# A transformer layer on one core: the first pass over the scores on 64 rows, two heads side by side in the row halves of TensorE

## The chip, the cores and the metric

The kernel runs on one core of a Trainium2 chip. The metric is the time of one execution on the device in microseconds, the median of several runs.

## The reference

One layer with a LayerNorm ahead of each half: `x = x + attention(LN(x))`, then `x = x + ffn(LN(x))`, with x of 2 x 2048 x 256 in float32. Attention has 16 heads of 16 dimensions, is causal, and q and k go through a rotary embedding:

```python
q = split_heads(x @ Wq.T + bq)          # k and v likewise
q, k = (rope(q), rope(k))
att = jnp.einsum('bhqd,bhkd->bhqk', q, k) / 4.0
att = jax.nn.softmax(jnp.where(mask, att, -jnp.inf), axis=-1)
y = jnp.einsum('bhqk,bhkd->bhqd', att, v)
```

The feed-forward part (256 to 704 to 256) rounds the input and the weights of each product to a block-wise FP4 grid: `fp4_linear(silu(fp4_linear(x, w_gate)) * fp4_linear(x, w_up), w_down)`.

## The kernel before, in words

**Tiling.** 4096 tokens are 32 tiles of 128 and 8 chunks of 512 (four a sequence). A unit `u` is a chunk of queries and a group of four heads: 8 x 4 = 32 units, in the order of chunks. A step is a unit and one tile of 128 keys, 320 in all. Everything is float32 but the score products. For these, q and k are each split into three bf16 parts (high, middle, low), and six products of parts stand below each other in the contraction: `Q_TERMS` and `K_TERMS` name them, 6 x 16 = 96 rows (`TERM_ROWS`), and 3 more rows (`ROWS` = 99) subtract the row's maximum, also in three parts, against three rows of ones.

**First pass (L766).** For each piece (unit, query tile, up to 512 keys; one head, or several where few keys are left) TensorE multiplies the 96 rows into one bank of PSUM, and on the diagonal adds the mask with an identity matmul (L770). VectorE reduces the bank to a maximum (L1096). When all pieces of a unit are done, VectorE splits the negated maxima in three (`place_maxima`, L1107 to L1122), TensorE turns them (L870), ScalarE copies them out (L1026), and SyncE places them with three DMAs in rows 96 to 98 of `q_mem` (L716).

**Second pass.** L784 computes the scores with keys on the partitions from all 99 rows, the maximum thus already subtracted; L787 adds the mask; ScalarE takes the exponential (L1037) into `prob`; and P·V (L805) multiplies by V, four heads side by side in four column quarters of the array (128 rows by 32 columns each), as float32 in two passes, so eight matmuls a step, all into bank 7 (`O_BANK`).

**The rest.** Projections (L817 with `WqkvT`), RoPE on GpSimd (L1362 to L1371) and in the first chunk on VectorE for every second tile, the splitting (`hi`, `mid`, `lo`), transposes of the parts (L863), their store to DRAM by SyncE (L687, one DMA of 768 KB for two tiles) and the deals, twelve DMAs a unit that bring each part into its rows of `q_mem` and `k_mem` (L698, L707). Feed-forward tiles (L812, L817, L906, L915) run between the attention of later chunks.

**What sets the order.** A planner (`Plan`) rehearses the whole program before it is built, with a duration for each step written in the code, and gives every step a number; each engine's program then emits its steps in that order (`in_time`). `Plan.through` also picks the bank for each use: of those free, the one that comes free first. `rehearse_maxima` keeps at most `S_IN_FLIGHT` = 4 pieces of the first pass between matmul and reduction, `rehearse_probabilities` at most three of the second. TensorE waits, in `take`, until the bank's last user has drained it. A first pass may run up to two units ahead of the second, since two sets of maxima exist.

## Time and profile before

| | before |
|---|---|
| median of 3 runs | 1479.56 us (1475.61 to 1482.19) |
| the profiled execution | 1482.4 us, of which the profile's span is 1480.6 |
| mean granted TensorE clock | 0.969 |
| TensorE matmul busy | 1364.8 us (92%), 8500 instructions |
| VectorE busy | 1111.1 us (75%), 2300 |
| ScalarE busy | 819.1 us (55%), 1724 |
| GpSimd busy | 496.4 us (34%), 552 |

Busy time is the time in which an instruction of the engine is under way. Matmuls are pipelined and their ends modelled, so what one matmul costs TensorE is read from the distance between starts. PE is TensorE, PEld its weight loads, DVE VectorE, ACT ScalarE, POOL GpSimd, SP SyncE. L766 is line 766 of the kernel.

### The profile page before, as it was taken

What the parts mean: (1) busy time and instruction counts of PE and PEld (TensorE: products, weight loads), DVE (VectorE), ACT (ScalarE), POOL (GpSimd) and SP (SyncE); (2) the same over time, 40 slices, a digit from 0 to 9 for tenths busy, and PEclk for the clock granted to TensorE, in tenths of its full rate; (3) what the DMA queues carried; (4) which work ended last, traced back from release to release, by engine and by line L of the source; (5) the groups of instructions that cost most, each with busy time, mean ns of one, the idle gap of its engine ahead of it and who ended that gap; (6) DMA issues with size and microseconds to landing.
All of it is one profiled execution on the core that took longest, in us unless ns stands there. A gap on an engine that the chain in (4) does not pass through costs nothing.

```text
span 1480.6 us, 23285 instructions
## 1 busy us (share of the span) xinstructions
PE 1364.8 (92%) x8500; PEld 675.7 (46%) x8500; DVE 1111.1 (75%) x2300; ACT 819.1 (55%) x1724; POOL 496.4 (34%) x552
## 2 busy tenths in 40 slices
PE   5669899899989999999989999999999999999986
PEld 2344344454444444444435545454345444444454
DVE  4688996889768797887527887878887987874373
ACT  1446466555556565655674555565665655667510
POOL 5743333424333451212212352542121122123345
PEclk9789999999999999999999999999999999999997
DMA  4323203111111101100011202120001000000000
GB/s 92 100 79 113 61 1 96 42 46 33 33 33 44 40 26 37 30 8 30 27 30 51 79 5 77 46 66 8 23 30 37 23 8 9 9 8 8 26 1 18
DMA packets 78457, 56.63 MB, mean 38 GB/s; under 512 B 12924, under 2 KB 78076, under 8 KB 78332
## 3 DMA queue, kind: packets, MB, share of 16 engines
q1 hardware_dynamic: 78344, 55.15, 12.8%
q8 instruction: 67, 1.10, 0.3%
q14 instruction: 46, 0.38, 0.1%
HBM read 37.95 MB, written 16.78 MB: 37 GB/s over the span
## 4 chain that ended last, share of the span: by engine, by line
PE 65%; DVE 21%; DMA 4%; issue 3%; ACT 3%; SPq 2%; POOL 2%; DVEq 0%; ACTq 0%; POOLq 0%
PE bank L817 15%; PE bank L805 14%; PE bank L784 12%; PE bank L766 11%; DVE piece_max L1096 10%; PE bank L915 5%; DMA a_mem<-in_L_attn_x 3%; ACT prob L1037 2%; PE bank L812 1%; PE bank L906 1%; PE bank L770 1%; PE bank L787 1%; DVE c_mem L1174 1%; PE bank L863 1%; DVE c_mem L1166 1%
## 5 line engine op out<-in xcount | busy, mean ns | idle before, releaser
L1037 ACT ACTIVATE prob<-bank 128x512 f32<-128x512 f32 (+3 forms) x1280 | 627.7, 537 | 411.4 <-PE bank L784 242.3
L1096 DVE TENSOR_REDUCE piece_max<-bank 128x1 f32<-128x512 f32 (+3 forms) x1120 | 703.9, 662 | 100.6 <-PE bank L766 56.6
L766 PE MATMUL bank<-k_mem,q_mem 96*128 96x512 bf16 (+3 forms) x1280 | 430.1, 352 | 18.6 <-DVE piece_max L1096 10.3
L784 PE MATMUL bank<-q_mem,k_mem 99*128 99x512 bf16 (+3 forms) x1280 | 434.9, 353 | 7.4 <-DVE piece_max L1096 5.7
L805 PE MATMUL bank<-prob,V 128*32 128x512 f32 (+3 forms) x2560 | 303.3, 546 | 2.4 <-ACT prob L1037 1.4
L784 PEld LDWEIGHTS bank<-q_mem,k_mem 99*128 99x128 bf16 x1280 | 123.8, 98 | 226.2 <-issue 140.9
L1324 POOL TENSOR_TENSOR c_mem<-c_mem 128x256 f32<-128x256 f32 (+2 forms) x72 | 82.4, 1145 | 407.9 <-DVE c_mem L1178 407.9
L766 PEld LDWEIGHTS bank<-k_mem,q_mem 96*128 96x128 bf16 x1280 | 125.8, 99 | 160.6 <-issue 71.1
L787 PE MATMUL bank<-mask_kq,ident_h 128*128 128x128 bf16 x512 | 110.7, 221 | 0.0
L770 PE MATMUL bank<-mask_qk,ident_h 128*128 128x128 bf16 x512 | 101.4, 224 | 0.0
L805 PEld LDWEIGHTS bank<-prob,V 128*32 128x32 f32 x2560 | 50.9, 109 | 97.1 <-issue 60.3
L1362 POOL TENSOR_TENSOR a_mem<-a_mem,sin_t 128x256 f32<-128x256 f32 x54 | 42.6, 810 | 138.6 <-DVE a_mem L1229 138.6
L817 PE MATMUL bank<-WqkvT,a_mem 128*128 128x512 f32 (+1 forms) x216 | 87.2, 528 | 0.8 <-ACT a_mem L998 0.6
L1327 POOL TENSOR_TENSOR c_mem<-c_mem 128x256 f32<-128x256 f32 (+2 forms) x72 | 82.7, 1148 | 3.6
L915 PE MATMUL bank<-WdT,c_mem 128*128 128x256 f32 x348 | 81.2, 383 | 1.2 <-ACT c_mem L1077 1.1
L817 PE MATMUL bank<-WgT,c_mem 128*128 128x352 f32 x232 | 81.3, 475 | 0.0
L817 PE MATMUL bank<-WuT,c_mem 128*128 128x352 f32 x232 | 79.0, 463 | 0.0
L1330 POOL TENSOR_TENSOR c_mem<-c_mem 128x256 f32<-128x256 f32 (+2 forms) x72 | 70.4, 978 | 3.9
L915 PEld LDWEIGHTS bank<-WdT,c_mem 128*128 128x128 f32 x348 | 64.7, 190 | 14.4 <-issue 4.7
L1382 POOL TENSOR_TENSOR c_mem<-c_mem,out_bias 128x256 f32<-128x256 f32 x29 | 21.0, 726 | 145.1 <-DMA c_mem<-in_L_attn_x 145.1
L1017 ACT ACTIVATE parts<-bank 128x1024 bf16<-128x1024 bf16 (+1 forms) x64 | 51.3, 812 | 25.9 <-PE bank L863 20.1
L787 PEld LDWEIGHTS bank<-mask_kq,ident_h 128*128 128x128 bf16 x512 | 50.6, 99 | 28.9 <-issue 5.6
(136 smaller groups left out, 1463.3 us busy)
## 6 DMA issues: line engine op xcount, KB each, us to landing
parts_dram<-parts SPq DMA_DIRECT2D x16, 768.0 KB, 4.3
q_mem<-parts_dram SPq DMA_DIRECT2D x192, 64.0 KB, 2.3
k_mem<-parts_dram SPq DMA_DIRECT2D x192, 64.0 KB, 2.3
c_mem<-in_L_attn_x SPq DMA_DIRECT2D x29, 128.0 KB, 2.1
out<-c_mem SPq DMA_DIRECT2D x29, 128.0 KB, 1.7
a_mem<-in_L_attn_x SPq DMA_DIRECT2D x27, 128.0 KB, 2.9
q_mem<-max_rows SPq DMA_DIRECT2D x96, 4.0 KB
k_mem<-in_L_attn_x SPq DMA_DIRECT2D x8, 128.0 KB, 2.9
```

The lines of the kernel that those rows point to most:

```text
L766: m = pe.matmul(o, q_rows(u)[0:TERM_ROWS, h, i * P:(i + 1) * P], k_rows(k0 // CHUNK, g)[0:TERM_ROWS, h, k0 % CHUNK:k0 % CHUNK + keys], sta ...
L770: m = pe.matmul(o[:, keys - P:keys], ident_h[:, :], mask_qk[:, :], start=False, stop=True)
L784: mm = pe.matmul(b[:, off:CHUNK], k_rows(j // TPC, g)[:, h, (j % TPC) * P:(j % TPC + 1) * P], q_rows(u)[:, h, off:CHUNK], start=True, stop ...
L787: mm = pe.matmul(b[:, off:off + P], ident_h[:, :], mask_kq[:, :], start=False, stop=True)
L805: mm = pe.matmul(O[32 * h:32 * h + 32, off:CHUNK], V[:, of % V_SLOTS, j % TPC, v0:v0 + 32], prob[:, (GROUP * m + h) % NP, off:CHUNK], star ...
L817: m = pe.matmul(b[:, 0:width], src[:, d * P:(d + 1) * P], w[:, d, lo:lo + width], start=(d == 0), stop=(d == DK - 1))
L915: m = pe.matmul(b[:, 0:D], hT[0:DOWN[j], j * P:(j + 1) * P], WdT[0:DOWN[j], j, :], start=(j == 0), stop=(j == len(DOWN) - 1))
L1037: act.activation(prob[:, n % NP, off:CHUNK], bank_of("st", n)[:, off:CHUNK], ACT.Exp, scale=SCALE).then_inc(drained("st", n)[0], 1)
L1096: dve.tensor_reduce(piece_max[:, u % 2, h0:h0 + len(heads), slot], src.rearrange("p (h k) -> p h k", k=keys), AX.X, ALU.max).then_inc(drai ...
L1324: pool.tensor_tensor(a, a, b, ALU.add).then_inc(done, 1)
L1327: pool.tensor_tensor(a, a, b, ALU.subtract).then_inc(done, 1)
L1330: pool.tensor_tensor(dst.rearrange("p (n f) -> p n f", f=FP4_BLOCK), a.rearrange("p (n f) -> p n f", f=FP4_BLOCK), v["scale"][0:rows, 0:nb ...
```

## The change

The first pass leaves two of the six products out (those with a low part), so it works on 64 rows: high x high, middle x middle, high x middle and middle x high. The second pass keeps all six. Since what the first pass finds is only subtracted inside the exponential and divides out again, the result stays what it was. Of the four heads of a group, heads 0 and 1 keep these 64 rows in partitions 0 to 63 and heads 2 and 3 in partitions 64 to 127; two matmuls, one in each half of the array's rows, go into two neighbouring banks, and one reduction takes both banks. A batch holds all four heads: two such pairs in a row, thus four banks, or one pair where two heads' keys fit in a bank. The masks of a batch follow after its matmuls.

Around that: the rows move (`BLOCK_AT`, `MAX_AT`); heads 2 and 3 have 29 rows of zeros in the second pass, which VectorE clears once; q, k, their weights and bias are laid out with the two heads of a pair innermost (`h=2`), so RoPE and the copies of weights go over other strides; the parts are stored by 14 DMAs of 64 KB for two tiles, and the deals take blocks of 32 rows by two heads; the maxima are placed with two DMAs. The planner knows pairs of banks (`pairs`, `take`), charges 70 ns for each change of the array's mode, counts 470 and 1800 ns instead of 550 and 1600 for a DMA's turn and landing, and prefers a batch by 1500 ns that can begin directly behind a P·V.

```diff
-S_IN_FLIGHT, ST_IN_FLIGHT = 4, 3
+S_IN_FLIGHT, ST_IN_FLIGHT = 2, 3
...
-HANDOVER_NS, DMA_TURN_NS, DMA_NS = 130, 550, 1600
+HANDOVER_NS, DMA_TURN_NS, DMA_NS, MODE_NS = 130, 470, 1800, 70
...
+BLOCK_AT = ((0, 32, 64), (64, 96, 0))
+MAX_AT = (96, 32)
+ROWS = (99, 128)
+ZEROS = (32, 64)
+PAIR_ROWS = ((0, 64), (64, 128))
...
+        if engine == "pe":
+            ns += MODE_NS * (mode != self.mode)
+            self.mode = mode
...
+    def pairs(self):
+
+        return [[b, b + 1] for b in self.bank_free if b % 2 == 0 and b in self.spare and b + 1 in self.spare]
...
-        for n, (u, i, heads, k0, keys, slot, masked) in enumerate(pieces):
-            yield [("deal k", u, 5)] + ([("place", u - 2, 2)] if u >= 2 else [])
-            if n >= S_IN_FLIGHT:
-                yield [("drain", "s1", n - S_IN_FLIGHT)]
...
+            for n in batch:
+                if n >= S_IN_FLIGHT:
+                    yield [("drain", "s1", n - S_IN_FLIGHT)]
+                yield plan.pairs
+                free.append(plan.take(("s1", n), min(plan.pairs(), key=lambda two: max(plan.bank_free[b] for b in two))))
+            yield free
+            for n in batch:
+                heads = pieces[n][2]
+                plan.do("pe", ("s1", n), 0.427 * len(heads) * keys + 10, *needs, *free, ("masks",), mode="rows")
...
+    plan.start(rehearse_maxima(), lambda begins: 1500 if plan.mode == "columns" and begins <= plan.engine_free["pe"] else SOONER_NS["s"])
...
+                for n, (o, part, d, row) in enumerate(stores):
...
+                    sp.dma_start(dst.rearrange("b r h t -> b (r h) t"),
+                                 parts[:, (part * 2 + o) * DK + d, :]).then_inc(parts_stored, 16)
...
-                        m = pe.matmul(o, q_rows(u)[0:TERM_ROWS, h, i * P:(i + 1) * P],
-                                      k_rows(k0 // CHUNK, g)[0:TERM_ROWS, h, k0 % CHUNK:k0 % CHUNK + keys],
-                                      start=True, stop=not masked)
...
+                    for n in batch:
+                        take("s1", n)
+                        b = plan.bank["s1", n]
+                        for j, h in enumerate(pieces[n][2]):
+                            for a in range(2):
+                                lo, hi = PAIR_ROWS[a]
+
+                                m = pe.matmul(bank[b + a][:, j * keys:(j + 1) * keys],
+                                              q_heads(u)[lo:hi, 2 * a + h, i * P:(i + 1) * P],
+                                              k_heads(k0 // CHUNK, g)[lo:hi, 2 * a + h, k0 % CHUNK:k0 % CHUNK + keys],
+                                              start=(j == 0), stop=not masked)
...
-                    dve.tensor_reduce(piece_max[:, u % 2, h0:h0 + len(heads), slot],
-                                      src.rearrange("p (h k) -> p h k", k=keys), AX.X,
...
+                    src = banks[:, b:b + 2, 0:some * keys].rearrange("p a (h k) -> p a h k", h=some)
+                    dve.tensor_reduce(of_tile[:, :, heads[0]:heads[0] + some], src, AX.X,
                                       ALU.max).then_inc(drained("s1", n)[0], 1)
...
+                dve.memset(q_mem[ZEROS[0]:ZEROS[1], :, 2:4, :], 0.0).then_inc(q_zeroed, 1)
```

## Rows read from the trace of the kernel before

**Rows 1.** Stretches: busy us per engine (instructions), TensorE clock, DMA share, GB/s.

```profile
102.00:1400.00 1298.00, 1248.09 (x7986) 599.00 (x7984) 1008.75 (x2071) 774.84 (x1632) 397.35 (x442) 0.99 0.12 35
0.00:102.00 102.00, 59.49 (x300) 36.03 (x300) 60.65 (x134) 31.68 (x62) 59.09 (x71) 0.83 0.37 98
1400.00:1480.60 80.60, 57.22 (x218) 40.65 (x218) 41.67 (x97) 12.62 (x31) 39.93 (x39) 0.85 0.05 15
```

**Rows 2.** The page: the chain that ended last, by engine.

```profile
PE 65%; DVE 21%; DMA 4%; issue 3%; ACT 3%; SPq 2%; POOL 2%; DVEq 0%; ACTq 0%; POOLq 0%
```

**Rows 3.** Groups by shape: busy us, mean ns of one, idle before.

```profile
L1096 DVE TENSOR_REDUCE piece_max<-bank 128x1 f32<-128x512 f32 x896 | 578.3, 677 | 66.8 <-PE bank L766 56.6 <-PE bank L770 8.9
L766 PE MATMUL bank<-k_mem,q_mem 96*128 96x512 bf16 x896 | 341.1, 383 | 11.1 <-DVE piece_max L1096 7.7 <-DVE c_mem L1266 1.2 <-issue 0.9
...
L1096 DVE TENSOR_REDUCE piece_max<-bank 128x1 f32<-128x384 f32 x128 | 66.8, 546 | 14.4 <-PE bank L770 13.5
```

**Rows 4.** TensorE in order of time: start us, length us, instruction; from 901.5.

```profile
901.50 0.38 PE L784 MATMUL bank<-q_mem,k_mem 99*128 99x512 bf16 x1
...
902.15 0.22 PE L787 MATMUL bank<-mask_kq,ident_h 128*128 128x128 bf16 x1
...
903.72 0.59 PE L817 MATMUL bank<-WqkvT,a_mem 128*128 128x512 f32 x1
904.15 0.38 PE L784 MATMUL bank<-q_mem,k_mem 99*128 99x512 bf16 x1
...
904.43 0.38 PE L766 MATMUL bank<-k_mem,q_mem 96*128 96x512 bf16 x1
904.74 1.06 PE L805 MATMUL bank<-prob,V 128*32 128x512 f32 x8
905.73 0.48 PE L817 MATMUL bank<-WqkvT,a_mem 128*128 128x256 f32 x1
```

**Rows 5.** TensorE in order of time, 613.4 us: 384 columns.

```profile
613.37 0.33 PE L766 MATMUL bank<-k_mem,q_mem 96*128 96x384 bf16 x1
613.53 0.22 PE L770 MATMUL bank<-mask_qk,ident_h 128*128 128x128 bf16 x1
```

**Rows 6.** TensorE in order of time, 107.8 us: small matmuls with weight loads.

```profile
107.84 0.61 PE L863 MATMUL bank<-ident_h,a_mem 128*128 128x128 bf16 x8 [0.66 <-issue]
108.28 0.28 PE L766 MATMUL bank<-k_mem,q_mem 96*128 96x256 bf16 x1
108.40 0.22 PE L770 MATMUL bank<-mask_qk,ident_h 128*128 128x128 bf16 x1
```

**Rows 7.** VectorE in order of time, from 1049 us and at 1100 us.

```profile
1049.55 0.69 DVE L1096 TENSOR_REDUCE piece_max<-bank 128x1 f32<-128x512 f32 x1 [1.40 <-PE bank L766]
...
1054.00 0.69 DVE L1096 TENSOR_REDUCE piece_max<-bank 128x1 f32<-128x512 f32 x1 [0.94 <-PE bank L766]
...
1100.28 0.68 DVE L1096 TENSOR_REDUCE piece_max<-bank 128x1 f32<-128x512 f32 x1
1100.88 0.32 DVE L1113 CAST max_parts<-neg_max 128x16 bf16<-128x16 f32 x1
```

**Rows 8.** Stretches, 1000 to 1300 us: all engines, then L1096 alone.

```profile
sum 300.00, PE 296.88 PEld 135.96 DVE 254.91 ACT 179.20 POOL 60.74; mean PE 98.96 PEld 45.32 DVE 84.97 ACT 59.73 POOL 20.25
...
1100.00:1200.00 100.00, 65.14 (x104) 1.00 0.08 23
sum 300.00, DVE 197.09; mean DVE 65.70
```

**Rows 9.** SyncE's DMA issues in order of time, the first chunk.

```profile
56.12 0.38 SPq L687 DMA_DIRECT2D parts_dram<-parts  x1
...
60.45 2.68 SPq L698 DMA_DIRECT2D q_mem<-parts_dram  x6
```

**Rows 10.** The page: DMA issues with KB of each and us to landing.

```profile
parts_dram<-parts SPq DMA_DIRECT2D x16, 768.0 KB, 4.3
```

**Rows 11.** SyncE's queue: what it waited for, us in total, times, longest.

```profile
SPq L716 <- ACT max_rows L1026: 345.5, 28, 24.9
```

317 lines of the change are left out of this document (192 added, 125 removed).

## The prediction, made before the changed kernel was run

> **What bounds the kernel now.** I read the span by stretches first, then the chain of work that ended last, then the groups by shape, then single instructions in order of time. The first query shows one long stretch: from 102 to 1400 us TensorE is busy 1248 of 1298 us at a granted clock of 0.99, so full speed, while VectorE has 1009, ScalarE 775 and GpSimd 397 us [rows 1]. Before 102 us and after 1400 us TensorE is busy 59 of 102 and 57 of 81 us; these ends are set by latencies and hardly touched here. The chain agrees: 65% TensorE, 21% VectorE [rows 2]. A busy TensorE could still be slow inside, because modelled durations overlap, so I take starts. From 901.50 us three score matmuls of 512 columns follow each other, and what comes after them starts at 902.15: 0.217 us each, without a hole [rows 4]. TensorE's order of work is full, and what shortens it shortens the span, until something else is late. The nearest to that is VectorE's chain of maxima: from 1000 to 1300 us it spends 66% on them and some 19% more on other work [rows 7, 8].
>
> **The first pass, what it costs now.** 1280 matmuls (L766): 896 of 512 columns [rows 3], and by the code 128 each of 384, 256 and 128 (four heads of 32 units), at the edge of the triangle. By their starts: 512 columns 0.217 us [rows 4], 384 columns 0.16 us (613.37 to 613.53 [rows 5]), 256 columns 0.12 us and, by the neighbouring 128-column rows, 0.06 us [rows 6]. Sum 896 x 0.217 + 128 x (0.16 + 0.12 + 0.06) = 194 + 44 = 238 us.
>
> **What it costs after.** The same columns go out as 320 batches of four matmuls (one batch for each unit, query tile and chunk of keys, so four heads), with heads 0 and 1 of a pair in rows 0 to 63 and heads 2 and 3 in rows 64 to 127. No row of this trace shows two row halves at once. The nearest is P·V (L805), four column quarters: eight matmuls of 512 f32 columns start at 904.74 and the next instruction at 905.73, so 0.99 us, where one whole-array f32 matmul of 512 columns takes 0.43 (903.72 to 904.15) [rows 4]. Two times 0.43 covers eight quarters, so quarters do run together. The bounds are 2 x 0.217 = 0.43 us for a full batch if halves run together, and 4 x 0.217 = 0.87 if they don't. I take the first, as the P·V row is nearest, plus 0.03 for the start of the second half (between 0 and the 0.055 us at which L863 puts out matmuls that each have a weight load of 128 columns: eight from 107.84 to 108.28 [rows 6]). The same 0.055 is the floor of a narrow matmul: the 128-column batch, four matmuls with four loads, gets 4 x 0.055 = 0.22 and hence nothing. Sum 224 x 0.465 + 32 x (0.35 + 0.26 + 0.25) = 104 + 28 = 132 us. Gain 238 - 132 = 106 us.
>
> **Changes of array mode.** Row halves, column quarters and whole array are three shapes of the array. The trace prices the change between the last two: L766 at 904.43 to L805 at 904.74 is 0.31 where 0.22 is its own, so 0.09 going in; coming out 0.99 - 2 x 0.43 = 0.13, less a few hundredths that lie between the two passes of P·V, so 0.10 [rows 4]. Before, 320 P·V steps pay both. Each batch now adds one more change if it stands directly behind a P·V (quarters, halves, whole), and two if it stands alone: 320 x 0.1 = 32 us to 320 x 0.2 = 64 us. The planner gets a bonus of 1500 ns for the first case, but only when a batch is ready at that moment; with half of them so placed, 45 us. The masks (L770) keep their number and their 0.055 us, in whole mode. TensorE net: 106 - 45 = 61 us less. The Trainium skill (TensorEngine Tiling (Array Packing), Key Properties) says that changing the mode drains the engine; it gives no price. The 0.09 us of P·V is this case's, and for halves no run here shows it yet.
>
> **VectorE.** 1120 reductions of up to 512 columns become 576 of up to 1024 over two banks. 677 ns for 512 and 546 for 384 [rows 3] give 1.02 ns per column; neighbours that follow each other start 0.60 us apart (1100.28 to 1100.88 [rows 7]), so about 0.07 us of each is fixed. 544 fewer are 38 us less work; it lies off the path now, since TensorE is the late one, and is worth nothing by itself. It gets five memsets of 4096 bf16 columns on 32 partitions; between 0 and 8 times the 0.60 us of a 512-column row, that is 4.8 us each. VectorE is idle 41 us before 102 [rows 1], which hides what of it falls there; the others come under TensorE's work. 0 taken, at most 5 us if the first attention waits.
>
> **Queues.** Stores of the parts become 14 of 64 KB for a pair of tiles where one of 768 KB stood [rows 10]: +208 issues; placing the maxima takes 64 and not 96, the ones 8 and not 4. Six q deals take 2.68 us of SyncE's queue [rows 9], 0.45 each, so 13 more stores hold it 6 us. The deals keep their count (384). Once, at the start, this is on the path: the second store of chunk 0 goes at 56.12 and the first deal at 60.45 [rows 9]; 14 stores then end at 62.4, and with the 4.3 us to landing of rows 10 the deals go at about 65 to 67. I take +5 us (0 to 10). Later it hides: SyncE's queue sits 345 us waiting for maxima [rows 11], and the first pass runs up to two units ahead of the second. Bias and weights copied in an interleaved order are some eight short ScalarE copies before 102 us; RoPE keeps its elements, with a pair innermost: 0, at most 5 us at the start on GpSimd, which is busy 59 of 102 us there [rows 1].
>
> **The wait it turns into.** Before, each bank had its own reduction and four were in flight, so a new matmul needed one drained bank. Now two pairs must be drained before the next batch is planned, and behind a waiting batch all of TensorE's later work is queued. VectorE in turn has nothing of the first pass to do until the first pair is filled. A full batch is two reductions of 1024 columns, 2 x (1.04 + 0.07) = 2.2 us, then 0.1 for the change of mode, 0.22 for the first pair, about 0.15 for the handover (0.38 us modelled less 0.22 [rows 4]) and the rest of what TensorE has in hand, 0 to 1.0 us (a P·V step) : 2.7 to 3.7, middle 3.2 us. Other work of VectorE is 0.7 us per batch: 19% of the 3.85 us that four reductions take now at 104 in 100 us [rows 8]. If it fits into the pause, 3.2; if all of it is in series, 3.9. TensorE's own cadence falls from 3.85 to 3.85 - 0.435 + 0.03 + 0.15 = 3.6 us. So the two are close, and I allow 15 us of new idle time on top of the 50 us that TensorE has from 102 to 1400 [rows 1]; even now two of the three reductions of rows 7 begin after a wait for score matmuls, of 1.40 and 0.94 us.
>
> **Sum.** The profiled execution has a span of 1480.6 and took 1482.4 us, 3 above the median of 1479.6. 1482.4 - 61 + 5 + 15 = 1441, less 3: 1438 us.
>
> **Rivals.** (a) Everything fits: all batches behind a P·V, the deals no later, no new idle time: 1479.6 - 106 + 32 = about 1405, and 1395 if halves start without the 0.03. For it: VectorE gets 38 us lighter. Against: a batch is ready only when four banks are. Chance 0.16. (b) The reductions take nearly all back: cadence near 3.8 us, TensorE waits for pairs. 1479.6 - 10 + 5 = about 1475. Chance 0.12. The Trainium skill has a rule for this (same page, PSUM Bottleneck): tiling speeds TensorE but not the draining of PSUM. By it the time would be that of (b); the trace leaves VectorE 290 us free from 102 to 1400 [rows 1], so I don't make it the likeliest. (c) Slower by one mechanism: reduction and filling strictly in series, with pairs blocked by other users of one of their banks (bank 7 belongs to the output, so only three pairs exist). It decides from a cadence of 3.85 us on. At 4.1 the 224 full batches cost 224 x 0.25 = 56 us more: about 1535. Against it: the planner knows these rules and orders the work by them. Chance 0.12. (d) The halves don't run together: no gain of 106 but the 45 us of mode changes: 1479.6 + 45 + 5 = about 1530. Against it: the quarters of P·V. Chance 0.06.
>
> **How the numbers follow.** The forecast, 1410 to 1465 with 1438 in the middle, has 0.54. 0.5% of this kernel is 7.4 us, about what can be told from no change. Faster: 0.54 + 0.16 and nothing of (b), 0.70. Same: (b), 0.12. Slower: (c) and (d), 0.18. The range reaches 1395 for (a) and, upwards, over (b) and the cheap end of (c), to 1490; the rest of (c) and (d), some 0.15, is left out.
>
> **What would show it.** Right: in the order of TensorE, two L766 successors with the same head number start within 0.06 us, the next two 0.22 later, and the batch spans 0.45 to 0.5 us before what follows; halves after quarters lose about 0.1. TensorE's sum for them falls by about 100 us; idle time before it for VectorE's maxima grows by 10 to 20 us. The first P·V starts at 105 to 110 us and not 102. Wrong: a batch of 0.87 us means (d). TensorE busy under 90% with VectorE over 85% in 1000 to 1300 us means (b) or (c). A mode change of halves that costs 0.2 rather than 0.1 us takes back 32 to 64 us more, and a change of 0.05 gives 20 us.

## The result, and the profile after

| | before | after |
|---|---|---|
| median of 4 runs each | 1480.88 us (1475.61 to 1483.96) | 1562.39 us (1560.09 to 1562.98) |
| ratio, 95% interval | | 1.055 (1.052 to 1.059) |
| profile's span | 1480.6 us | 1558.0 us |
| mean granted TensorE clock | 0.969 | 0.947 |

The change makes the kernel 82 us slower; I had forecast 42 us faster, with a range that ends at 1490. In the changed kernel L841 is the first pass, L854 its mask, L870 the second pass's scores, L891 P·V, L1196 the reductions, L1136 the exponential, L755 the stores of the parts, L768 and L777 the deals, L788 the placing of the maxima.

The page of after, busy time by engine, then the chain that ended last, by engine and by line:

```profile
PE 1333.2 (86%) x8399; PEld 595.0 (38%) x8500; DVE 1085.8 (70%) x1761; ACT 815.9 (52%) x1729; POOL 484.9 (31%) x552
...
PE 53%; DVE 16%; SPq 10%; ACT 8%; issue 5%; DMA 5%; POOL 2%; another core or an unknown queue 1%; POOLq 0%; DVEq 0%; ACTq 0%
```

TensorE and VectorE both have less work than before, in a longer span. TensorE's share of the chain falls from 65% [rows 2] to 53%, SyncE's queue rises from 2% to 10%. So the work got shorter, as forecast, and the waits grew by more. The stretches answer to [rows 1, 8]: the start; from the first P·V (123 us) to the last exponential; and 1000 to 1300 us, then the same with L1196 alone. Columns are as in [rows 1].

```profile
0.00:102.00 102.00, 51.53 (x244) 30.82 (x244) 59.18 (x105) 27.91 (x58) 58.50 (x72) 0.78 0.35 89
123.00:1466.70 1343.70, 1214.72 (x7905) 520.50 (x8004) 975.39 (x1540) 770.12 (x1633) 389.69 (x439) 0.98 0.13 35
1000.00:1300.00 300.00, 276.00 (x1753) 113.52 (x1772) 242.52 (x364) 168.08 (x352) 73.45 (x83) 0.99 0.11 29
...
1000.00:1300.00 300.00, 173.74 (x152) 0.99 0.11 29
```

In the middle TensorE is busy 276 of 300 us (92%) and not 297, VectorE 243 (81%) and not 255. Neither is full: no engine has become the bound. The groups of after, with the idle time ahead of each and what ended it:

```profile
L1196 DVE TENSOR_REDUCE piece_max<-banks 128x2 f32<-128x1024 f32 (+2 forms) x576 | 649.2, 1158 | 107.3 <-PE banks L841 64.8
...
L870 PEld LDWEIGHTS banks<-q_mem,k_mem 99*128 99x128 bf16 (+1 forms) x1280 | 116.6, 97 | 335.3 <-ACT prob L1136 135.1
L841 PE MATMUL banks<-k_mem,q_mem 64*128 64x512 bf16 (+3 forms) x1280 | 182.1, 358 | 38.1 <-DVE piece_max L1196 21.9
```

The surprise is the second line: the matmuls that wait longest are not those of the first pass, which I had expected to wait for its pairs of banks. They are the second pass's scores, for a bank that ScalarE has not emptied. By waits (total us, times, longest), weight loads of the second pass, before and after:

```profile
PEld bank L784 <- ACT prob L1037: 6.4, 17, 0.8
```

```profile
PEld banks L870 <- ACT prob L1136: 135.1, 256, 1.0
PEld banks L841 <- DVE piece_max L1196: 38.4, 46, 4.9
```

**Needed time and stalls.** Since ends of matmuls are modelled, I split TensorE's span by starts. For each pair of neighbouring shapes the pitch at the tenth percentile, or a shorter one where it was, counts as needed; what a pitch has above that is a stall, put to the instruction that came late. It is a reckoning of my own from the trace. The columns of the first pass and of the second pass's scores hold to 7 us when shapes are grouped otherwise; the totals do not. With a matmul's place in its burst taken as part of its shape, needed time comes to 1292 before and 1228 after, stalls to 182 and 323. All in us:

| kernel | needed | of it first pass | stalls | ahead of first pass | of second pass's scores | of all else |
|---|---|---|---|---|---|---|
| before | 1272.6 | 248.5 | 201.3 | 34.7 | 20.3 | 146.3 |
| after | 1182.1 | 151.1 | 368.9 | 48.4 | 96.5 | 224.0 |

The needed time falls by 90.5 us, stalls rise by 167.6 (by the other grouping 64 and 141); the difference, 77, is that of the spans. Only 14 us of the rise stand ahead of the first pass itself; 76 stand ahead of the second pass's scores, and 78 (56) ahead of all else; of the 168, 20 lie before 200 us.

### The profile page after: what moved, and what is told of

Its sections match the earlier page's. It is cut to its first block, busy times and chain, and to the rows that moved or that the text cites. A ratio compares the mean times of both kernels' runs of the same rounds, so it can differ in the third digit from the quotient of the medians.

```text
span 1558.0 us, 22901 instructions
## 1 busy us (share of the span) xinstructions
PE 1333.2 (86%) x8399; PEld 595.0 (38%) x8500; DVE 1085.8 (70%) x1761; ACT 815.9 (52%) x1729; POOL 484.9 (31%) x552
## 4 chain that ended last, share of the span: by engine, by line
PE 53%; DVE 16%; SPq 10%; ACT 8%; issue 5%; DMA 5%; POOL 2%; another core or an unknown queue 1%; POOLq 0%; DVEq 0%; ACTq 0%
PE banks L903 14%; PE banks L891 12%; PE banks L870 9%; DVE piece_max L1196 8%; SPq L755 6%; PE banks L841 6%; ACT prob L1136 5%; PE banks L1001 5%; DMA a_mem<-in_L_attn_x 2%; PE banks L854 2%; ACT parts L1116 1%; SPq L768 1%; SPq L777 1%; PE banks L992 1%; PE banks L873 1%
## 5 line engine op out<-in xcount | busy, mean ns | idle before, releaser
L1136 ACT ACTIVATE prob<-banks 128x512 f32<-128x512 f32 (+3 forms) x1280 | 624.1, 537 | 430.1 <-PE banks L873 190.7
L1196 DVE TENSOR_REDUCE piece_max<-banks 128x2 f32<-128x1024 f32 (+2 forms) x576 | 649.2, 1158 | 107.3 <-PE banks L841 64.8
L870 PE MATMUL banks<-q_mem,k_mem 99*128 99x512 bf16 (+6 forms) x1179 | 367.1, 353 | 53.4 <-ACT prob L1136 27.6
L891 PE MATMUL banks<-prob,V 128*32 128x512 f32 (+3 forms) x2560 | 305.0, 549 | 5.2 <-ACT prob L1136 3.0
L870 PEld LDWEIGHTS banks<-q_mem,k_mem 99*128 99x128 bf16 (+1 forms) x1280 | 116.6, 97 | 335.3 <-ACT prob L1136 135.1
L841 PE MATMUL banks<-k_mem,q_mem 64*128 64x512 bf16 (+3 forms) x1280 | 182.1, 358 | 38.1 <-DVE piece_max L1196 21.9
L841 PEld LDWEIGHTS banks<-k_mem,q_mem 64*128 64x128 bf16 x1280 | 41.9, 94 | 179.6 <-issue 134.2
L873 PE MATMUL banks<-mask_kq,ident_h 128*128 128x128 bf16 x512 | 107.4, 222 | 2.8 <-issue 1.7
L1001 PE MATMUL banks<-WdT,c_mem 128*128 128x256 f32 x360 | 89.8, 402 | 1.9 <-ACT c_mem L1176 1.5
L903 PE MATMUL banks<-WqkvT,a_mem 128*128 128x512 f32 (+1 forms) x216 | 88.5, 535 | 0.7 <-ACT a_mem L1097 0.6
L903 PE MATMUL banks<-WgT,c_mem 128*128 128x352 f32 x240 | 85.4, 480 | 1.6 <-ACT c_mem L1163 1.1
L891 PEld LDWEIGHTS banks<-prob,V 128*32 128x32 f32 x2560 | 50.8, 108 | 90.9 <-issue 54.8
L1116 ACT ACTIVATE parts<-banks 128x1024 bf16<-128x1024 bf16 x64 | 50.8, 811 | 34.4 <-PE banks L949 24.4
```

The lines of the kernel that those rows point to most:

```text
L841: m = pe.matmul(bank[b + a][:, j * keys:(j + 1) * keys], q_heads(u)[lo:hi, 2 * a + h, i * P:(i + 1) * P], k_heads(k0 // CHUNK, g)[lo:hi, 2 ...
L870: mm = pe.matmul(b[:, off:CHUNK], k_heads(j // TPC, g)[0:rows, h, (j % TPC) * P:(j % TPC + 1) * P], q_heads(u)[0:rows, h, off:CHUNK], star ...
L873: mm = pe.matmul(b[:, off:off + P], ident_h[:, :], mask_kq[:, :], start=False, stop=True)
L891: mm = pe.matmul(O[32 * h:32 * h + 32, off:CHUNK], V[:, of % V_SLOTS, j % TPC, v0:v0 + 32], prob[:, (GROUP * m + h) % NP, off:CHUNK], star ...
L903: m = pe.matmul(b[:, 0:width], src[:, d * P:(d + 1) * P], w[:, d, lo:lo + width], start=(d == 0), stop=(d == DK - 1))
L1001: m = pe.matmul(b[:, 0:D], hT[0:DOWN[j], j * P:(j + 1) * P], WdT[0:DOWN[j], j, :], start=(j == 0), stop=(j == len(DOWN) - 1))
```

## The experiments

The theory that I went in with, A in the expectations, was that batches cost the time: the order of work and the banks that they hold. C was that it is the changes of array mode. Each kernel below has its own median in us and its ratio to the kernel before, measured beside it, with a 95% interval; a loss in us is that ratio less 1, times 1480. A difference of two losses is good to about 3 to 6 us.

**One part at a time.** `b_batch` is the kernel before with only the batches: 96 rows, the whole array, one store, but pairs of neighbouring banks, two pairs at a time, one reduction of two banks and the changed planning. Its pieces also come in another order, by chunk of keys and then by head, as in the changed kernel.

```diff
+        for batch in batches:
...
+            for n in batch:
+                if n >= S_IN_FLIGHT:
+                    yield [("drain", "s1", n - S_IN_FLIGHT)]
+                yield plan.pairs
+                free.append(plan.take(("s1", n), min(plan.pairs(), key=lambda two: max(plan.bank_free[b] for b in two))))
+            yield free
...
+            plan.start(rehearse_reducing(batch, masked))
```

> The kernel before, with its 96 rows and whole-array matmuls, its one store and its layout, but with the first pass in the changed kernel's batches: two pairs of neighbouring banks in a row, one reduction over two banks, at most two pieces in flight. Theory A (the batches: four of seven banks taken and given back in pairs, so the second pass and the first wait for banks) expects a loss of 60 to 130 us against before, with the waits of the second pass for the exponentials grown as in the changed kernel. Theory B (the 14 stores on SyncE's queue) and theory C (changes of the array's mode) have nothing to act here and expect within 15 us of before.

Measured 1586.46 us, ratio 1.073 (1.071 to 1.075): +107 us. Batches alone cost more than the whole change, with no halves and no new mode changes in it. Its needed time is that of before (1267.9 us), its stalls are 309.8. From 1000 to 1300 us, and the second pass's wait:

```profile
1000.00:1300.00 300.00, 282.81 (x1715) 132.50 (x1714) 232.38 (x350) 163.79 (x341) 73.81 (x81) 1.00 0.09 26
```

```profile
PEld banks L831 <- ACT prob L1084: 67.8, 133, 1.3
```

VectorE is down to 232 us of 300 and ScalarE to 164 (179 before [rows 8]): every engine has gaps.

`b_stores` is the kernel before with its one store of two tiles cut in twelve:

```diff
+    STORES = PART_CHUNKS
...
-                sp.dma_start(dst, parts[:, :, :]).then_inc(parts_stored, 16)
+                for n in range(STORES):
...
+                    sp.dma_start(dst[:, n:n + 1, :], parts[:, n:n + 1, :]).then_inc(parts_stored, 16)
```

> The kernel before with one edit: the store of the parts for two tiles goes out as 12 DMAs of 64 KB and not as one of 768 KB, and the planner counts them. Theory B (SyncE's queue holds deals and maxima back behind the stores) expects 30 us or more over before, at least 5 of them before the first P·V. Theory A and theory C expect within 10 us of before, most of it in the start.

Measured 1504.66 us, ratio 1.017 (1.015 to 1.019): +25 us, a little under the 30 that theory B asked for. The first P·V comes at 110.5 us instead of 102.1. From the first P·V to the last exponential, then from there to the end, before and then `b_stores`:

```profile
102.07:1400.51 1298.44, 1248.22 (x7986) 599.02 (x7984) 1008.68 (x2070) 775.04 (x1633) 397.35 (x442) 0.99 0.12 35
1400.51:1480.60 80.09, 57.02 (x216) 40.63 (x216) 41.67 (x97) 12.35 (x31) 39.93 (x39) 0.85 0.04 14
```

```profile
110.49:1408.97 1298.48, 1251.22 (x7958) 596.31 (x7956) 1009.11 (x2058) 769.86 (x1629) 390.82 (x436) 0.98 0.12 34
1408.97:1501.90 92.93, 59.04 (x226) 41.15 (x226) 43.84 (x98) 12.94 (x30) 38.82 (x39) 0.81 0.05 14
```

The middle is as long as before, 1298 us. The loss lies at both ends: 8 us ahead of the first P·V and 13 behind the last exponential.

**The planner's two new rules, in the changed kernel.** `a_oldsel` takes away the new choice of a single bank (which prefers one whose neighbour is in use), `a_nobonus` the 1500 ns for a batch behind a P·V:

```diff
-        b = min(self.spare, key=lambda b_: (max(self.bank_free[b_], self.engine_free.get("pe", 0.0)),
-                                               b_ ^ 1 in self.spare, self.bank_free[b_]))
+        b = min(self.spare, key=lambda b_: self.bank_free[b_])
```

> The changed kernel with the planner's old choice of a bank (the one that has been free longest, whatever its neighbour does). In the changed kernel bank 6 carries 471 of the 1280 second-pass matmuls, because it has no partner. Theory A expects a gain of 10 to 30 us on the changed kernel, with less waiting of the second pass for the exponentials. Theories B and C expect within 5 us of the changed kernel.

```diff
-    plan.start(rehearse_maxima(), lambda begins: 1500 if plan.mode == "columns" and begins <= plan.engine_free["pe"] else SOONER_NS["s"])
+    plan.start(rehearse_maxima(), lambda begins: SOONER_NS["s"])
```

> The changed kernel without the planner's bonus of 1500 ns for a batch directly behind a P·V. Theory C (mode changes are what costs) expects it slower by 5 to 15 us, since some 60 of 93 such places are lost at 0.1 us each and more. Theory A expects it faster by 5 to 20 us, since batches are no longer put ahead of second-pass work that is due.

1556.41 us (1.051, 1.049 to 1.053) and 1551.66 us (1.048, 1.045 to 1.051), so 6 and 10 us less than after. The first is smaller than I expected, and no more than the two intervals leave open. The second bears on the mode changes: without the rule, 50 batches and not 93 stand directly behind a P·V and the changes rise from 1174 to 1222, and the kernel is still 10 us faster, as theory A expected and theory C did not. Neither is the cause.

**What in the batch?** Two steps back from `b_batch`. `b_four` keeps the batch of four but takes any four banks, each with its own reduction, four and not two in flight; `b_two` does the same with two at a time.

```diff
-                yield plan.pairs
-                free.append(plan.take(("s1", n), min(plan.pairs(), key=lambda two: max(plan.bank_free[b] for b in two))))
+                for a in range(2):
+                    m = 2 * n + a - S_IN_FLIGHT
+                    if m >= 0:
+                        yield [("drain", "s1", m // 2, m % 2)]
+                    yield lambda: plan.spare
+                    free.append(plan.take(("s1", n, a), [min(plan.spare, key=lambda b: plan.bank_free[b])]))
```

> As b_batch (the kernel before with batches of four heads), but each of the four matmuls goes into any free bank, is reduced by itself, and gives its bank back by itself; four banks in flight. Theory A1 (what costs is that four banks are asked for at once, before the batch may start) expects within 12 us of b_batch, 1575 to 1598 us. Theory A2 (what costs is the neighbouring pair, held until one reduction over both banks is over) expects at least 40 us less than b_batch, below 1546.

> As b_four, but two heads and two banks at a time. Theory A1 expects about half of the loss of b_four, so 1510 to 1545 us, and the second pass waits less for the exponentials. Theory A2 expects no difference from b_four of over 10 us.

1570.34 us (1.063, 1.060 to 1.065) and 1549.52 us (1.049, 1.047 to 1.051). `b_four` lies between what A1 and A2 gave, 5 us below the range of A1. Neighbour pairs and the shared reduction are thus only 15 of the 107 us, and even two at a time cost 72 us, where the expectation ended at 1545. Halving the batch takes 20 of 92 us away and leaves 72: its size does not explain them.

`b_less` asks what one bank is worth: the kernel before, with six and not seven for the scores. `b_470` changes only two of the planner's constants (and has the reciprocal of the row sums wait for their last reader, which the new order needs), to see how much a mere reshuffle moves.

```diff
-    plan.run(lambda: O_BANK in plan.spare)
+    plan.run(lambda: O_BANK in plan.spare and 6 in plan.spare)
     plan.spare.remove(O_BANK)
+    plan.spare.remove(6)
```

> The kernel before with bank 6 given to nobody once attention begins: six banks in place of seven for everything but the output. Theory A-banks (the changed kernel lacks banks) expects 40 us or more over before, since a batch that holds four takes about that from the others. Theory A-grain (four matmuls in a row, asked for in one piece, make TensorE's order lumpy, and ScalarE and VectorE run dry between) expects within 15 us of before.

```diff
-HANDOVER_NS, DMA_TURN_NS, DMA_NS = 130, 550, 1600
+HANDOVER_NS, DMA_TURN_NS, DMA_NS = 130, 470, 1800
```

> The kernel before with the planner's two DMA durations of the changed kernel (470 and 1800 ns for 550 and 1600) and nothing else that moves time (the reciprocal of the row sums waits for its last reader). All theories expect within 10 us of before; a larger difference would say how much a time depends on the order that the planner happens to find.

1510.67 us (1.023, 1.020 to 1.025): one bank is 34 us, between what the theories said. 1483.78 us (1.004, 1.003 to 1.006): this other order moves 6 us. It is one order among many, so it sets no bound on what a reshuffle can do.

**The pace.** What `b_two` still shares with `b_batch` is how it is planned. Before, a piece and its reduction are one job of the planner, and the next piece is planned only when the reduction has its place. In the changed kernel the reduction is a job by itself. `b_one` makes only that change: one bank, one reduction, no batch.

```diff
-            yield from plan.through(("s1", n), 0.427 * len(heads) * keys + 57 * len(heads) * masked,
-                                    "dve", 64 + 1.0 * len(heads) * keys, [("masks",)], [])
...
+            plan.do("pe", ("s1", n), 0.427 * len(heads) * keys + 57 * len(heads) * masked, ("deal k", u, 5), free, ("masks",))
+            plan.start(rehearse_reducing(n, len(heads) * keys))
```

> The kernel before, one bank and one reduction at a time as it was, but the reduction is a step of its own in the planner, so the next piece of the first pass may take its bank and be multiplied before the reduction of the last one is placed: up to four really ahead. Theory P (lost pacing, banks filled too early) expects 20 to 45 us over before. Theory G (only the size of the batch counts) expects within 8 us of before.

1564.51 us, ratio 1.058 (1.054 to 1.061): +85 us from the same instructions in another order, about two to four times what theory P gave. Then `b_one_paced` puts the pace back: the next piece is planned only once this one's matmul is behind the planner's clock, and the reduction has the first pass's priority.

```diff
-            plan.start(rehearse_reducing(n, len(heads) * keys))
+            plan.start(rehearse_reducing(n, len(heads) * keys), SOONER_NS["s"])
+            yield [("s1", n)]
```

> b_one (1565 us) with one line back: the next piece of the first pass is planned only after the matmul of the last one has ended in the plan, and its reduction has the first pass's precedence. Theory P expects the 85 us gone, within 10 us of before. If b_one's loss came from the reduction being a step of its own, it stays above 1540.

1478.14 us, ratio 1.001 (1.000 to 1.002): all 85 us are back. The two kernels differ in these two lines, and both need about the same time of TensorE (1270.6 and 1274.0 us); stalls are 287.9 against 195.3. The waiting for the matmul and the precedence of the reduction came back together; no run parts them. From 1000 to 1300 us, `b_one`, then `b_one_paced`:

```profile
1000.00:1300.00 300.00, 279.66 (x1700) 130.03 (x1698) 249.89 (x501) 160.59 (x332) 65.31 (x71) 0.98 0.09 26
```

```profile
1000.00:1300.00 300.00, 296.89 (x1847) 135.41 (x1848) 255.63 (x513) 179.39 (x377) 63.06 (x66) 1.00 0.06 18
```

TensorE gets through 1847 matmuls, as against 1700, and ScalarE through 377 instructions, as against 332. The last stretch shows where the work went, `b_one` from its last first-pass matmul to its last exponential, and the same of before:

```profile
1316.00:1475.00 159.00, 153.86 (x951) 68.30 (x949) 56.08 (x127) 114.29 (x249) 46.15 (x47) 1.00 0.03 10
```

```profile
1326.00:1400.00 74.00, 72.19 (x440) 33.06 (x432) 29.11 (x62) 50.79 (x112) 23.69 (x24) 1.00 0.03 10
```

In `b_one` the first pass ends at 1316 us, earlier than before, and leaves 159 us of second pass behind it and not 75: 83 us more, which is about the loss. A first pass that isn't held back runs ahead, and the second pass, whose chain of scores, exponential and P·V gets fewer turns, is alone at the end. It doesn't show as a wait for ScalarE's bank, which is 19.8 us here:

```profile
PEld bank L797 <- ACT prob L1050: 19.8, 59, 0.8
```

This picture is `b_one`'s, and `b_two`'s (146 us left behind the last matmul of the first pass). In `b_batch` the first pass ends late and only 57 us follow it, in `b_four` 97, in the changed kernel 99. So that batches lose by a first pass that runs ahead is shown for one and two banks at a time, not for the changed kernel's batch of four.

**Late banks.** `b_four` plans its banks one by one, so it holds the first while it waits for the fourth; `b_four_late` waits until four are there, and until the batch before is reduced, and takes all at once; `b_four_paced` adds the two lines of `b_one_paced`.

```diff
+            m = 2 * batch[-1] + 1 - S_IN_FLIGHT
+            if m >= 0:
+                yield [("drain", "s1", m // 2, m % 2)]
+            yield lambda: len(plan.spare) >= 2 * len(batch)
             for n in batch:
                 for a in range(2):
-                    m = 2 * n + a - S_IN_FLIGHT
-                    if m >= 0:
-                        yield [("drain", "s1", m // 2, m % 2)]
-                    yield lambda: plan.spare
                     free.append(plan.take(("s1", n, a), [min(plan.spare, key=lambda b: plan.bank_free[b])]))
```

> As b_four (1570 us), but the four banks of a batch are taken together once all four are free, so none is held empty while others are waited for. Theory H (banks held empty) expects 20 to 40 us less than b_four. Theory G expects within 8 us of b_four.

> b_four_late (1543 us) with the same line: the next batch is planned only after the last one's matmuls. Theory P with H expects 1500 to 1530 us; what then remains over before (1479) is the batch of four itself. Theory G, that the size alone costs, expects it unchanged within 8 us of b_four_late.

1542.53 us (1.043, 1.039 to 1.046) and 1500.88 us (1.014, 1.012 to 1.017). The wait of the second pass's weight loads for ScalarE, `b_four`, `b_four_late`, `b_four_paced`:

```profile
PEld banks L833 <- ACT prob L1086: 63.8, 114, 1.3
```

```profile
PEld banks L833 <- ACT prob L1086: 15.6, 41, 0.8
```

```profile
PEld banks L834 <- ACT prob L1087: 18.8, 45, 0.9
```

Banks held empty by a batch are most of what the second pass's scores waited for: with late taking, their wait falls from 63.8 to 15.6 us, P·V's wait for the exponentials rises from 35.5 to 50.8, and the time falls by 30. The two lines of the pace give 42 more, through other stalls (266.6 to 220.6 us in all). In the profiled executions, which differ by 46 us, 2 of them lie ahead of the first P·V, 31 from there to the last exponential and 14 behind it. The second pass left behind the first pass's last matmul stays at 76 and 72 us, so what the pace mends here is not what it mends in `b_one`.

**The stores, in the changed kernel.** `a_stores` has two stores for two tiles instead of 14, from a buffer whose planes are then combined by the deals; `a_stores2` differs in the order of the letters in the deals' source, that is in which dimension is outermost.

```diff
-                                 parts_dram[k, Q_PLANES[block], 0, rows, :].rearrange("s (r h) t -> s r (h t)", h=2)).then_inc(q_dealt[u % Q_SLOTS], 16)
+                                 parts_dram[k, Q_PLANES[block], 0, rows, :].rearrange("s (r h) t -> r s (h t)", h=2)).then_inc(q_dealt[u % Q_SLOTS], 16)
...
-                                 parts_dram[k, K_PLANES[block], 1, rows, :].rearrange("s (r h) t -> s r (h t)", h=2)).then_inc(k_dealt[g], 16)
+                                 parts_dram[k, K_PLANES[block], 1, rows, :].rearrange("s (r h) t -> r s (h t)", h=2)).then_inc(k_dealt[g], 16)
```

> The changed kernel with 2 store DMAs for two tiles in place of 14: the three parts as before, and the high part once more as a fourth plane, so that each block of 32 rows is two planes; the deals stay twelve a unit. Theory B (the stores are the smaller share of the loss, 25 us as in b_stores) expects 15 to 35 us less than the changed kernel, 1527 to 1547 us, with the first P·V about 5 us earlier. A theory that the batches alone make the loss expects within 8 us of the changed kernel.

> As a_stores, 2 stores for two tiles, but each deal walks the 16 rows outermost and the two planes innermost, so its 32 packets of 2 KB spread over the DMA engines. In a_stores 384 such packets took 18 us, from 531 to 549 us, two at a time. Theory B expects the deals to land in 1.5 to 2 us again and the kernel 15 to 35 us faster than the changed one, 1527 to 1547 us. If the time stays above 1600, the second plane's order was not the cause of a_stores' loss.

1720.16 us (1.164, 1.162 to 1.167), against 1534.61 us (1.038, 1.036 to 1.040). The first deserves its rows; SyncE's issues in order of time, then stretches (TensorE, its loads, VectorE, ScalarE, GpSimd, clock, DMA share, GB/s), both of `a_stores`:

```profile
531.00 3.94 SPq L766 DMA_DIRECT2D q_mem<-parts_dram  x6
534.99 4.62 SPq L775 DMA_DIRECT2D k_mem<-parts_dram  x6
```

```profile
531.00:549.00 18.00, 15.20 (x86) 5.00 (x85) 17.19 (x29) 10.58 (x21) 10.48 (x11) 1.00 0.12 45
549.00:552.00 3.00, 2.41 (x19) 0.72 (x17) 2.96 (x4) 2.40 (x5) 2.00 (x3) 1.00 0.00 0
```

and the deals of one unit in after:

```profile
489.00:495.00 6.00, 3.23 (x18) 0.68 (x18) 2.33 (x4) 3.26 (x7) 3.54 (x4) 0.92 0.61 165
```

A DMA share of 0.12 for 18 us is what two of 16 engines give when they are busy all the time: by it a source with two planes outermost ran on two engines, at 45 GB/s, where the deals of after reach 165. With 16 rows outermost the kernel is 26 us faster than after, which is what the 14 stores cost, less what the new deals do. Here too the middle has no part in it (1346 us from the first P·V to the last exponential, 1344 in after): 9 us lie ahead of it and 17 behind. The new deals take longer: six hold SyncE's queue 3.84 us at the start of `a_stores2`, as against 2.68 [rows 9].

```profile
62.66 3.84 SPq L766 DMA_DIRECT2D q_mem<-parts_dram  x6
```

So its first P·V comes at 113.6 us, between before's 102.1 and after's 123.0. The Trainium skill (DMA: Bandwidth & Descriptors, Why a DMA increments its semaphore by 16 and not by 1) says that the number of engines follows from the sizes of the outermost dimensions of both sides, as their largest common divisor up to 16; the trace agrees, with 0.12 for two planes.

**Putting it together.** `a_best` and `a_best2` are `a_stores` and `a_stores2` with any banks, taken late, one pair of halves at a time; `a_four_paced` is `a_stores2` with four late banks, the pace, the old choice of a single bank and row sums in two buffers; `a_last` lets it have more in flight.

```diff
-                batches.append(list(range(len(pieces), len(pieces) + len(heads))))
+                batches += [[n] for n in range(len(pieces), len(pieces) + len(heads))]
```

> The changed kernel with 2 stores, with pairs of heads in row halves but two banks at a time, any two banks, taken only when both are free, each reduced by itself, three in flight, and the old choice of a bank; the reciprocal of the row sums waits for its last reader. Theory A1 with B expects the losses of b_batch and b_stores undone for the most part and the halves' gain of some 100 us less 640 changes of mode kept: 1440 to 1500 us. If the changes of mode (theory C) are what eats the gain, it stays at 1500 us or above.

> As a_best (row halves, two banks at a time, any two, reduced each by itself, three in flight, 2 stores), with the deals of a_stores2. Theory A (either form) with B expects 1465 to 1510 us: b_two's loss of 70 remains in part, the halves give some 100, and 640 pairs in place of 320 batches cost up to 60 more in changes of mode.

```diff
+            yield lambda: len(plan.spare) >= 2 * len(batch)
...
+            plan.start(rehearse_reducing(batch, masked), SOONER_NS["s"])
+            yield [(("masked" if masked else "s1"), batch[-1])]
```

> The changed kernel with 2 stores, batches of four into any four banks taken together once all are free, each bank reduced by itself, the old choice of a bank, the reductions with the same precedence as the batch, and the next batch planned only after the last one's matmuls; row sums in two buffers. Theories P and H together expect 1490 to 1520 us, below a_stores2 (1535); theory G expects 1530 or more.

```diff
-S_IN_FLIGHT, ST_IN_FLIGHT = 4, 3
+S_IN_FLIGHT, ST_IN_FLIGHT = 5, 4
-SOONER_NS = dict(a=0, s=50, st=0, pv=-100, place=0, norm=200, c=(50, -2000))
+SOONER_NS = dict(a=0, s=-200, st=0, pv=-100, place=0, norm=200, c=(50, -2000))
```

> a_four_paced (1507 us) with five banks of the first pass and four of the second allowed in flight, and the first pass 200 ns later in precedence instead of 50 sooner. If the second pass is what starves, 1470 to 1505 us, at best level with before; if not, within 8 us of a_four_paced.

1740.15 us (1.177, 1.175 to 1.179), again with two planes outermost; 1550.35 us (1.048, 1.046 to 1.050), a miss: 16 us worse than `a_stores2`, with a needed time of 1246.7 us where `a_stores2` needs 1203.0, since single pairs change the mode more often, 1578 times and not 1170; 1507.02 us (1.018, 1.014 to 1.022); and 1525.71 us (1.032, 1.030 to 1.033), a miss too: 19 us slower, where one theory expected a gain and the other no change. So the changed kernel can be mended from 1562 to 1507 us, but none of these beats the kernel before. The wait of the second pass's weight loads for ScalarE, `a_stores2`, then `a_four_paced`:

```profile
PEld banks L868 <- ACT prob L1134: 131.5, 239, 1.0
```

```profile
PEld banks L870 <- ACT prob L1136: 19.2, 58, 0.8
```

112 us of this wait are gone, and the time falls by 30. The largest wait in the list was thus not the measure of the loss: when it went, most of it came back as other waits. The stretch 1000 to 1300 us, `b_four_paced` and then `a_four_paced`:

```profile
1000.00:1300.00 300.00, 291.89 (x1771) 132.61 (x1770) 253.83 (x502) 169.64 (x357) 64.92 (x69) 1.00 0.08 24
```

```profile
1000.00:1300.00 300.00, 286.31 (x1840) 117.59 (x1869) 256.06 (x519) 179.56 (x380) 67.22 (x72) 0.99 0.10 27
```

With the halves TensorE gets more matmuls through in that stretch, 1840 to 1771 (ScalarE 380 to 357), but over the whole kernel they are no faster: 26 against 21 us over before. The first P·V comes at 112.9 us and not at 100.6; from there to the last exponential the two take 1317 and 1319 us.

## Why the prediction was wrong

**Where in the span.** The profiled executions, in us: the first P·V, from there to the last exponential, from there to the end, how much second pass follows the last matmul of the first, and for how long the granted clock was at the lower of its two levels (1.2 and not 2.4 GHz).

| kernel | first P·V | to last exponential | behind it | second pass alone | lower clock |
|---|---|---|---|---|---|
| before | 102 | 1298 | 80 | 75 | 92 |
| after | 123 | 1344 | 91 | 99 | 164 |
| `b_batch` | 102 | 1392 | 91 | 57 | 120 |
| `b_four` | 102 | 1372 | 90 | 97 | 96 |
| `b_four_late` | 103 | 1350 | 89 | 76 | 133 |
| `b_four_paced` | 101 | 1319 | 75 | 72 | 75 |
| `b_one` | 104 | 1371 | 91 | 159 | 160 |
| `b_one_paced` | 100 | 1296 | 80 | 75 | 89 |
| `a_stores2` | 114 | 1346 | 74 | 90 | 130 |
| `a_four_paced` | 113 | 1317 | 79 | 89 | 154 |

Of the 77 us between the spans of before and after, 21 lie ahead of the first P·V, 45 in the middle and 11 behind the last exponential. The clock is a rival that no run tests. TensorE at half the clock for L us loses at most L/2, so it can be up to 36 of the 77 us in after, 36 of the 89 that `b_one_paced` gets back and 29 of the 46 from `b_four_late` to `b_four_paced`, but only 2 of the 83 by which the span of `b_four` is longer than that of before. So a batch of four loses without it, and how much of the other losses the clock carries on stays open.

**How the 82 us add up.** The parts follow as differences of neighbouring kernels; they were measured in this order only, and need not be the same in another. The second step holds all of the change that is in neither of the others, the planner's two new rules (6 and 10 us, above) among it:

| step | kernels | predicted | measured |
|---|---|---|---|
| batches of two pairs (new waits) | before to `b_batch` | +15 | +107 |
| 64 rows in halves, mode changes, layout, planner's rules | `b_batch` to `a_stores2` | -61 | -51 (needed -65, stalls +14) |
| 14 stores and their deals | `a_stores2` to after | +5 | +26 |
| sum | | -41 | +82 |

**The step that failed is "the wait it turns into"**: 15 us, and it measured 107 (`b_batch`). I had asked whether a batch can be filled in the time in which its reductions run, found 3.6 us of TensorE against 3.2 to 3.9 us, and took the difference for all there was. I priced the batch as a matter of throughput, and looked for its wait at its own door. In the trace of after the first pass waits only 14 us longer, about the 15 I had allowed, and the rest falls on others. From 1000 to 1300 us it gives out 328 matmuls, as against 344: four in 3.66 us, and not 3.49, where I had forecast a shorter turn. The runs split the 107 us in four steps: 21 for a batch of four by itself (`b_four_paced`), 42 for the lost pace, with the reductions' precedence (to `b_four_late`), 30 for banks held empty until the fourth is there (to `b_four`), 15 for neighbour pairs and the shared reduction (to `b_batch`). Each step is one order found by the planner. My sentence that "the planner knows these rules and orders the work by them" was the argument against (c), and it is wrong in a way that the diff would have let me see: the change moves the reductions out of the job that plans the pieces, and with that a brake goes, worth 85 us by `b_one`. The rows of before could have made me ask: two of three reductions wait for score matmuls [rows 7], so the first pass was not issued as early as its banks allowed, and I read that as VectorE being nearly late.

**The first pass itself: right.** By starts it needs 97 us less (248.5 to 151.1), changes of mode behind it included; without them 119, as reckoned below, where 106 were predicted. TensorE of after in order of time; start, length, instruction:

```profile
1058.87 0.60 PE L870 MATMUL banks<-q_mem,k_mem 99*128 99x512 bf16 x2 [1.47 <-DVE piece_max L1196]
1059.40 0.60 PE L841 MATMUL banks<-k_mem,q_mem 64*128 64x512 bf16 x4
1059.94 0.39 PE L870 MATMUL banks<-q_mem,k_mem 128*128 128x512 bf16 x1
1060.26 1.07 PE L891 MATMUL banks<-prob,V 128*32 128x512 f32 x8
1061.26 0.28 PE L841 MATMUL banks<-k_mem,q_mem 64*128 64x128 bf16 x4
1061.48 0.40 PE L854 MATMUL banks<-mask_qk,ident_h 128*128 128x128 bf16 x4
```

A full batch is 0.54 us to its successor (59.40 to 59.94): two times 0.22 for the halves together, and 0.10 for the change of mode, inside the 0.465 + 0.1 of the sum. The two halves of a pair start 3 ns apart, so the 0.03 for the second half was not needed. Rival (d), halves one after the other, would have given 0.87 and is refuted. A batch of 128 columns takes 0.22 us with its change of mode: its four matmuls start at 0, 3, 66 and 69 ns, and the mask 148 ns later. So halves run together there too, in 0.12 us without the change; that 0.22 is also four times the 0.055 of my floor is luck.

**Mode changes: the price right, the count too low.** The 0.10 us stands in the rows above. I supposed half of the 320 batches directly behind a P·V; by the order of TensorE's work it is 93, so 29%, and the changes rise from 646 to about 1174, so 53 us at 0.1 each, for 45 predicted. The 97 us already bear a part of this: the 151.1 hold the change that follows each of 320 batches, 32 us, and the 248.5 those of 114 matmuls directly ahead of a P·V, 10 us. Without changes the first pass falls from 238 to 119 us, so by 119; less 53 that is 66, and the needed time of the whole second step (`b_batch` to `a_stores2`) falls by 65, or by 79 with the other grouping. The prediction's net, 61 us less of TensorE, was thus about right.

**VectorE: right.** The 448 reductions of 1024 columns take 1218 ns each, and where two follow each other they end within 2.34 us, so the second starts 1.12 after the first, as the 1.11 of the forecast:

```profile
1056.46 2.34 DVE L1196 TENSOR_REDUCE piece_max<-banks 128x2 f32<-128x1024 f32 x2
...
1059.84 2.96 DVE L1196 TENSOR_REDUCE piece_max<-banks 128x2 f32<-128x1024 f32 x3 [1.03 <-PE banks L841]
...
1064.08 2.36 DVE L1196 TENSOR_REDUCE piece_max<-banks 128x2 f32<-128x1024 f32 x2 [1.29 <-PE banks L841]
```

VectorE is 25 us lighter in all (1111.1 to 1085.8), for 38 predicted; the five memsets, put at nothing, take 1.77 us each. The rule that tiling doesn't speed the draining of PSUM (the Trainium skill, TensorEngine Tiling (Array Packing), PSUM Bottleneck) comes out right only in that the gain is gone. The time is 87 us above what (b) gave by it, and the drain is no bound: VectorE is at 81% in the middle, below the 85% of before. Rival (b) would have needed it above, and by the test that I had set (TensorE below 90% with VectorE above 85%) neither (b) nor (c) shows; with TensorE at 92% and VectorE at 81% what I saw was a third thing, gaps on both.

**Queues: five times too low.** Predicted +5 us, once, at the start; measured +26 in the changed kernel and +25 by `b_stores`, about 9 of it at the start and the rest behind the last exponential. SyncE's queue in after, at the start:

```profile
63.95 3.35 SPq L755 DMA_DIRECT2D q_dram<-parts  x6
67.34 5.34 SPq L755 DMA_DIRECT2D k_dram<-parts  x8
76.97 2.66 SPq L768 DMA_DIRECT2D q_mem<-q_dram  x6
...
101.00 3.39 SPq L755 DMA_DIRECT2D q_dram<-parts  x6
104.43 5.47 SPq L755 DMA_DIRECT2D k_dram<-parts  x8
112.01 3.10 SPq L788 DMA_DIRECT2D q_mem<-max_rows  x4
```

14 issues hold the queue 8.7 us (63.95 to 72.68), not 6: a store to DRAM takes some 0.6 us of it and not the 0.45 of a deal [rows 9], which I had used. This train also begins at 63.95, where before's one store goes at 56.12 [rows 9], and the first deal goes at 76.97 and not at 65 to 67. And I had moved only one train of stores past the deals. The next train goes from 101 to 110, and the maxima (L788) stand behind it until 112. The wait that ends last is another: ScalarE may refill `parts` only when the last of the 14 stores has landed, and TensorE's next matmuls wait for that copy:

```profile
114.49 2.92 ACT L1116 ACTIVATE parts<-banks 128x1024 bf16<-128x1024 bf16 x4 [3.29 <-DMA k_dram<-parts]
```

```profile
117.06 0.40 PE L841 MATMUL banks<-k_mem,q_mem 64*128 64x128 bf16 x4 [3.10 <-ACT parts L1116]
```

So the first P·V comes at 123 us and not at 105 to 110. "Later it hides" held for the middle of the span, in both kernels; it failed for the end, where `b_stores` loses 13 us and `a_stores2` to after 17. What the stores change there was not followed.

**The rivals.** The outcome is beyond (c), 1535 us, whose sign was right and whose mechanism was not: the pairs, with the shared reduction, are the 15 us. The chance of slower, 0.18, was built from two mechanisms of TensorE and VectorE alone, and none of the order.

**What stays open.** Why a batch of four, paced and with late banks, still costs 21 us (its pieces also come in another order, which no run tests alone); why the pace is worth 85 us with single banks and 42 with four; and why the halves, which need 70 to 90 us less of TensorE, gain nothing once the order is mended (stalls 220.6 us in `b_four_paced`, 322.2 in `a_four_paced`). That a first pass that isn't held back leaves the second behind is shown by the stretches of `b_one` and by `b_one_paced`; through which instructions each us of it goes was not followed, and in the batches of four the loss doesn't look like that.

## What to carry to other kernels

Where an engine runs its work in a fixed order, price a change of that order by itself: here 85 us came and went with two lines that changed no instruction, about as much as the 97 us of saved matmuls. Ask of every buffer from when to when it is held empty, and who else waits for it, for the wait shows up with that other user. Don't take the longest wait in the list for the loss: here 112 us of it went for 30 us of time. When one DMA is cut into many, walk every other transfer of its queue past them, and whoever waits for the last landing, at each place where it is needed soon. Of the dimensions of a DMA, put the 16 rows outermost and not the two planes.

## What the runs showed of the hardware that I had not expected

- Deals with two planes as the outermost dimension moved 45 GB/s at a DMA share of 0.12, that of two of 16 engines; the same bytes with 16 rows outermost made the kernel 186 us faster (1720 to 1535).
- The issue of a store of 64 KB from SBUF to DRAM held SyncE's queue for about 0.62 us (14 in 8.7), that of a deal for 0.44 (six in 2.66), each in a row of its kind.
- Two row halves ran fully side by side, with starts 3 ns apart: four matmuls of 512 columns in 0.44 us, four of 128 in 0.12, and 0.10 more for the change of mode behind them.
